# A two-level Winograd-style matrix product: the four raw products moved to the front, and the outer weight sums made partly by adding DMAs in DRAM

## The reference

```python
base  = einsum('bsi,oi->bso', x, weight) + bias        # one weight, 2048 x 2048
low   = einsum('bsi,bri->bsr', x, lora_a[itok7])       # rank 16, one of 8 adapters per batch
delta = einsum('bsr,bor->bso', low, lora_b[itok7])
x = x + base + scale[itok7] * delta
w = L1_weight[itok14]                                  # one of 16 weights per batch
x = x + einsum('bij,bkj->bik', x, w)
```

## Time and profile before

| | us |
|---|---|
| median of 3 runs | 2579.33 (2576.03 to 2581.75) |
| the profiled execution's own time | 2576.68 |
| its span | 2574.9 |
| TensorE busy | 2557.1 (99% of the span) |
| VectorE busy | 2114.2 (82%) |
| ScalarE busy | 1386.3 (54%) |
| GpSimd busy | 764.6 (30%) |
| DMA | 686.19 MB, mean 266 GB/s |

### The profile page before, as it was taken

How to read it: one execution, slowest core, us unless ns; L and a number is a source line. 1 busy time by engine, 2 the same in 40 slices (tenths; PEclk the granted TensorE clock), 3 DMA queues, 4 the chain that set the end, 5 groups by cost and what they waited for, 6 DMA issues and landing times.

```text
span 2574.9 us, 35471 instructions
## 1 busy us (share of the span) xinstructions
PE 2557.1 (99%) x12250; PEld 2114.8 (82%) x12250; DVE 2114.2 (82%) x1926; ACT 1386.3 (54%) x1478; POOL 764.6 (30%) x614
## 2 busy tenths in 40 slices
PE   8999999999999999999999999999999999999999
PEld 7888888888888888878888888888888888888887
DVE  6568999997888999898788787788877887887865
ACT  3324333334344333467676676766766666766755
POOL 5554332332333324220230231311311312212312
PEclk9999999999999999999999999999999999999999
DMA  9996642963576637878678677787899999998986
GB/s 357 352 379 197 203 135 99 290 213 131 162 239 216 168 131 242 308 264 280 243 258 297 240 263 279 247 278 260 290 355 355 353 349 365 353 324 320 312 325 228
DMA packets 213714, 686.19 MB, mean 266 GB/s; under 512 B 23424, under 2 KB 31776, under 8 KB 213536
## 3 DMA queue, kind: packets, MB, share of 16 engines
q1 hardware_dynamic: 204032, 649.33, 70.0%
q0 software_dynamic: 9216, 33.56, 6.7%
q10 hardware_dynamic: 288, 1.05, 0.1%
HBM read 650.29 MB, written 100.66 MB: 292 GB/s over the span
## 4 chain that ended last, share of the span: by engine, by line
PE 92%; DVE 4%; DMA 2%; issue 1%; ACT 0%; SPq 0%; POOL 0%; DVEq 0%; ACTq 0%; POOLq 0%
PE acc L1294 18%; PE acc L1295 18%; PE acc L1296 18%; PE acc L1211 12%; PE acc L1213 12%; PE acc L1212 12%; DVE tx L1165 1%; DVE ws L1165 1%; PE acc L1228 1%; PE acc L1250 1%; DMA bias_s<-bias 1%; DMA xb<-x_sums 1%; DMA xst<-xt 0%; DVE acc L1154 0%; DMA xb<-x 0%
## 5 line engine op out<-in xcount | busy, mean ns | idle before, releaser
L1165 DVE TENSOR_TENSOR ws<-wb,ws 128x1024 fp32r<-128x1024 f32 x968 | 1257.0, 1325 | 284.0 <-ACT ws L1001 268.2
L1001 ACT CAST ws<-wb 128x1024 fp32r<-128x1024 f32 x968 | 990.9, 1050 | 778.3 <-PE acc L1296 450.7
L1294 PE MATMUL acc<-ws,ops 128*128 128x512 f32 (+1 forms) x2048 | 799.9, 391 | 2.6 <-DVE ops L1165 2.3
L1295 PE MATMUL acc<-ws,ops 128*128 128x512 f32 (+1 forms) x2048 | 797.6, 389 | 0.0
L1296 PE MATMUL acc<-ws,ops 128*128 128x512 f32 (+1 forms) x2048 | 797.2, 389 | 0.0
L911 POOL TENSOR_TENSOR wb<-wb,eye_s 128x128 f32<-128x128 f32 x384 | 332.2, 897 | 1145.5 <-DMA wb<-w 1144.9
L1211 PE MATMUL acc<-tx,ws 128*128 128x512 f32 x1600 | 623.5, 390 | 4.5 <-DVE tx L1165 2.4
L1212 PE MATMUL acc<-tx,ws 128*128 128x512 f32 x1600 | 622.5, 389 | 0.0
L1213 PE MATMUL acc<-tx,ws 128*128 128x512 f32 x1600 | 622.5, 389 | 0.0
L1294 PEld LDWEIGHTS acc<-ws,ops 128*128 128x128 f32 x2048 | 384.6, 188 | 82.5 <-issue 6.2
L1296 PEld LDWEIGHTS acc<-ws,ops 128*128 128x128 f32 x2048 | 384.5, 188 | 81.0
(11 more groups left out here) (67 smaller groups left out, 1021.0 us busy)
## 6 DMA issues: line engine op xcount, KB each, us to landing
wb<-w SPq DMA_DIRECT2D x816, 512.0 KB, 6.8
xb<-x SPq DMA_DIRECT2D x78, 512.0 KB, 5.7
xb<-x POOLq DMA_DIRECT2D x64, 512.0 KB, 8.8
y<-acc SPq DMA_DIRECT2D x32, 1024.0 KB, 10.4
wb<-w_sums SPq DMA_DIRECT2D x64, 512.0 KB, 7.9
out<-ost SPq DMA_DIRECT2D x128, 256.0 KB, 7.4
xst<-xt SPq DMA_DIRECT2D x60, 512.0 KB, 6.4
ystage<-y SPq DMA_DIRECT2D x60, 512.0 KB, 7.3
```

Of the source, the lines that this page charges most:

```text
L1001: eng.copy(hi, src).then_inc(s_hi, 1)
L1165: eng.tensor_tensor(lo, src, hi, ALU.subtract).then_inc(s_lo, 1)
L1294: eng.matmul(dst, yh, wh, start=begin, stop=False)
L1295: eng.matmul(dst, yh, wl, start=False, stop=False)
```

## The change

Five things change together.

1. The outer products run in another order: (group 0, k = 0), (0, 1), (1, 0), (1, 1), then k = 2 to 6 of group 0, then k = 2 to 6 of group 1. These first four take raw weight quarters.
2. Only the first of them is `Eight` (`PLAIN = (0,)`), so there are 8 + 13 x 7 = 99 steps.
3. The partial result of (1, 0) stands in slot 1 as "P", is stored in a new DRAM tensor `x_part` (4 blocks of 1 MB), and comes back to slot 2 before outer product (1, 3) adds to it (`part_back`).
4. Of the four outer weight sums GpSimd makes only two parts per tile place, each a difference of two raw tiles (a21 - a22 and a11 - a12 of the outer quarters). For the other three sums, SyncE copies a11 from DRAM to DRAM (`base_sum`, 16 copies of 512 KB) for sums 1 and 2, sum 3 starts from GpSimd's second difference, and 24 adding DMAs issued by GpSimd ("more", three rounds of eight, DRAM to DRAM, 512 KB each) add the rest. The copies are due from 74 us on, the adding DMAs from 104 us on, 6.5 us apart.
5. `MADE_EVERY` goes from 18 to 12 us.

```diff
-SLOT = ({"X": 0, "Y": 1, "Q": 2, "Z": 1}, {"X": 2, "Y": 1, "Q": 0, "Z": 1})
-TARGET = ("X", "Y", "Q", "X", "X", "Z", "X")
+ORDER = [(0, 0), (0, 1), (1, 0), (1, 1)] + [(g, n) for g in range(NG) for n in range(2, K)]
+GRP, NUM = zip(*ORDER)
+POS = {gn: q for q, gn in enumerate(ORDER)}
+SLOT = ({"X": 0, "Y": 1, "Q": 2, "Z": 1}, {"P": 1, "X": 2, "Y": 2, "Q": 0, "Z": 1})
+TARGET = (("X", "Y", "Q", "X", "X", "Z", "X"), ("P", "Y", "Q", "X", "X", "Z", "X"))
...
-MADE_AS = (2, 0, 1, 3)
+MADE = ((1, "m1", 0), (2, "m2", 3))
 MADE_FROM = 10.0
-MADE_EVERY = 18.0
+MADE_EVERY = 12.0
+ADD_FROM = 104.0
+ADD_EVERY = 6.5
...
-PLAIN = (0, 1)
+PLAIN = (0,)
...
-        for i, after in ((1, 3.0), (0, 6.0), (2, 9.0), (3, 12.0)):
-            loads.append((made_key(p) + after, "keep", (p, i)))
+        for n in range(2):
+            loads.append((made_key(p) + 3.0 + 3.0 * n, "keep", (p, n)))
+            loads.append((ADD_FROM - 30.0 + 4.0 * (8 * n + p), "base", (n + 1, p)))
...
-        for i, kind in enumerate(("m1", "m2", "m3", "m4")):
-            adds.append((made_key(p) + 3.0 * i, kind, (p,)))
+        for n in range(2):
+            adds.append((made_key(p) + 3.0 * n, MADE[n][1], (p,)))
+        for n in range(1, 4):
+            adds.append((ADD_FROM + ADD_EVERY * (8 * (n - 1) + p), "more", (n, p)))
...
+    for blk in range(4):
+        loads.append((ev_key(last_step(POS[1, 0], blk), 3) + 6.0, "store", (1, "P", blk)))
+        loads.append((t_of(BEGIN[POS[0, 6]] + 4) + 11.0 * blk, "back", (blk,)))
...
+        def sum_stored(eng, n, p):
+            if n == 0:
+                made_kept(eng, p, 0)
+            else:
+                eng.wait_ge(s_more[p], 16 * n)
...
             def load_made(p, i):
                 if p >= 2:
-                    made_kept(eng, p - 2, i)
-                    eng.wait_ge(s_pool, pool_no["m4", p - 2])
+                    eng.wait_ge(s_pool, pool_no[MADE[i // 2][1], p - 2])
+                    if i in (1, 2):
+                        made_kept(eng, p - 2, i - 1)
...
+            def base_sum(n, p):
+                eng.dma_start(w_sum(n, p), w_part(0, 0, p)).then_inc(s_base[n - 1], 16)
...
+            def part_back(blk):
+                stored(eng, 0, "Q", blk)
+                stored(eng, 1, "P", blk)
+                eng.dma_start(acc[:, SLOT[1]["X"], blk, :], x_part[blk]).then_inc(s_back[blk], 16)
...
+                if kind == "more":
+                    n, p = index
+                    if n == 3:
+                        made_kept(eng, p, 1)
+                    else:
+                        eng.wait_ge(s_base[n - 1], 128)
+                    if n > 1:
+                        eng.wait_ge(s_more[p], 16 * (n - 1))
+                    if n != 2:
+                        made_kept(eng, p, 0)
+                    eng.dma_start(w_sum(n, p), w_part(1, 0, p) if n == 2 else w_sum(0, p), accum_op=ALU.add,
+                                  max_dma_last_dim=4096).then_inc(s_more[p], 16)
+                    continue
...
-                elif kind in ("m1", "m2", "m3", "m4"):
+                elif kind in ("m1", "m2"):
                     p, = index
...
+                    i = 0 if kind == "m1" else 2
+                    made_loaded(eng, p, i)
+                    made_loaded(eng, p, i + 1)
+                    ins = eng.tensor_tensor(made_tile(p, 1 if i == 0 else 2), made_tile(p, i), made_tile(p, i + 1),
+                                            ALU.subtract)
...
                     elif k == 3 and opens:
-                        ev_done(eng, last_step(K * g, blk), ot)
+                        if g:
+                            eng.wait_ge(s_back[blk], 16)
+                        else:
+                            ev_done(eng, last_step(POS[g, 0], blk), ot)
```

More of the change, by code:

```diff
@@ L35 @@
 LEAD = 13.0
+XS_AHEAD = 6.0
 X_ROLE = {"b11": (0, 0), "b12": (0, 1), "b21": (1, 0), "b22": (1, 1)}
@@ L90 @@
 BEGIN = [STEPS.index((q, 0)) for q in range(NG * K)]
-MADE = [(role, h) for role in FORM[2].w_need for h in range(2)]
+TILES = [(role, h) for role in FORM[POS[0, 2]].w_need for h in range(2)]
 def last_step(q, blk):
@@ L364, in program @@
     for _, kind, index in adds:
-        if kind != "acc":
+        if kind not in ("acc", "more"):
             count += 1
@@ L374, in program @@
             for ot in range(4):
-                (fast if q % K in (0, 2) and i in FORM[q].first else slow).append((ev_key(s, ot), s, ot))
+                (fast if NUM[q] in (0, 2) and i in FORM[q].first else slow).append((ev_key(s, ot), s, ot))
     fast.sort()
@@ L555, in ev_done, with stored, free_slot @@
             eng.wait_ge(s_copy if (s, ot) in by_copy else s_ev, ev_no[s, ot])
+        def stored(eng, g, name, blk):
+            eng.wait_ge(s_y0[SLOT[g][name]][blk], 16 * STORES[g, name])
+        def free_slot(eng, g, name, blk):
+            if (g, name) in FREE_BEHIND:
+                stored(eng, *FREE_BEHIND[g, name], blk)
         def blk_view(slot, blk):
@@ L778, in _ @@
                     keep_made(*index)
+                elif kind == "base":
+                    base_sum(*index)
                 elif kind == "store":
                     store_y0(*index)
+                elif kind == "back":
+                    part_back(*index)
                 elif kind == "raw":
@@ L811, in _ @@
                         y0_stored(0)
+                        y0_stored(1)
+                        for blk in range(4):
+                            stored(eng, 0, "Q", blk)
                     elif b == 0:
@@ L856, in _ @@
                     v = w_tile(q, role, h).rearrange("p (s n) -> p s n", s=2)[:, :, 256 * h:256 * h + P]
-                    ins = eng.tensor_tensor(v, v, eye_s[:], ALU.add if UNIT[q % K] > 0 else ALU.subtract)
+                    ins = eng.tensor_tensor(v, v, eye_s[:], ALU.add if UNIT[NUM[q]] > 0 else ALU.subtract)
                 elif kind == "s1":
@@ L969, in _ @@
                         for blk in range(4):
-                            eng.wait_ge(s_y0[2][blk], 32)
+                            stored(eng, 1, "X", blk)
                     else:
@@ L1081, in _ @@
                     x, q, z = (blk_view(SLOT[g][name], blk)[:, :, cols] for name in ("X", "Q", "Z"))
-                    s = last_step(K * g + (3 if what == "z" else 4), blk)
+                    s = last_step(POS[g, 3 if what == "z" else 4], blk)
                     ev_done(eng, s, 2 * oh + 1)
@@ L1177, in _ @@
             for i in range(WARM):
-                eng.matmul(bank[0][:], tx[:, 0, 0, 0:P], tx[:, 0, 0, 0:512], start=True, stop=True)
+                eng.matmul(bank_at(0, 0)[:], tx[:, X_SLOT[0], 0, 0:P], tx[:, X_SLOT[0], 0, 0:512], start=True, stop=True)
             for blk in blocks:
@@ L1187, in _ @@
                         eng.wait_ge(s_key, 10)
-                        eng.matmul(bank[6][:, 0:NB], wide, put, start=True, stop=True).then_inc(s_put, 1)
+                        eng.matmul(order_at[:, 0:NB], wide, put, start=True, stop=True).then_inc(s_put, 1)
                     if blk == ("W", 1, 2):
```

132 lines of the change are left out of this document (66 added, 66 removed).

## The result

The changed kernel takes 2581.73 us (median of 20 runs, 2579.17 to 2584.23), the kernel before 2577.7 us (20 runs, 2576.03 to 2581.75). The ratio is 1.0014, with a 95% interval of 1.0008 to 1.0020. It is slightly slower, within the 0.2% that the prediction called no change. The forecast of 2567.4 us and the range up to 2577 us were wrong: one step less was bought, and it brought nothing. Its profiled execution has a span of 2578.8 us, 3.9 us over before.

What follows compares the result with a forecast made beforehand. TensorE was taken as the bound: matmul count times pace, plus its waits. −10.9 − 1.5 + 0.5 = −11.9 us took the median 2579.33 to 2567.4 us, range 2562 to 2577.

Steps and rivals of the forecast that it cites:

- One step less: Outer product 1 no longer plain: 48 matmuls fewer on TensorE at 0.2267 us each, −10.9 us.
- Sixteen GpSimd sums fewer: Early outer sums dropped, so VectorE runs freer between 33 and 70 us: −1.5 us, bounds 0 and −2.3.
- VectorE in outer product 1: VectorE's added splits and additions fit, 64.7 of 76 us busy: +0.5 us, bounds 0 and +3.
- GpSimd's list ahead of outer product 1: Second s2 behind all 16 differences and the last raw tile, near 108 us, still in time: 0 us, bound +3.
- Rival A: Last raw tile lands at 118 us or later, stalling TensorE 7 to 11 us: about 2576 us, chance 0.12.
- The copies: Sixteen DRAM copies; first eight land near 120 us, before the s4 behind the first adding DMA may start: covered.
- The adding DMAs: 24 adds into DRAM, 1.35 to 5.4 us each, fit the queue before outer product 5: 0 us, bound +6.
- Rival B: Slow DRAM adds stop GpSimd's list above 9.4 us each; at 12 us each, 2601 us, chance 0.13.
- The partial result: 4 MB stored and read back, the read starting some ten steps before its user: 0 us.
- C: Small new stalls in Sevens during busy DMA, VectorE losing 3 to 6 us in sum: 2571 to 2574, chance 0.15.

Runs made afterwards that it cites:

- Experiment 10: Changed kernel with early reads of the partial result and GpSimd's differences of tile places 5 to 7 on 8 of 1024 columns (result incomplete): 2569.77 us, before 2578.01.
- Experiment 2: Changed kernel with GpSimd's differences of tile places 5 to 7 on only 8 of 1024 columns (result incomplete): 2578.06 us, before 2578.03.
- Experiment 6: Changed kernel with early reads of the partial result, differences of places 5 to 7 at 176 to 207 us, adding DMAs from 185 us, copies moved along: 2614.09 us.
- experiment 4: Changed kernel with outer product 1 plain again, one step more, all else as changed: 2587.78 us, before 2578.03.
- experiment 3: Changed kernel with the partial result's reads some 50 us later and differences of places 5 to 7 on 8 of 1024 columns (result incomplete): 2575.31 us, before 2578.03.
- experiment 1: Changed kernel with the four 1 MB reads of the partial result issued some 50 us later: 2580.06 us, before 2578.03.
- experiment 5: Changed kernel with three reads of the partial result issued early, the fourth after the x saves of outer product (1, 2); full result: 2574.74 us, before 2578.2.
- experiment 8: Kernel before, plus four DRAM copies of 1 MB where the changed kernel reads the partial result; nothing waits for them: 2587.86 us, before 2578.33.
- experiment 7: Changed kernel with early reads, differences of places 5 to 7 due at 143, 168 and 224 us, adding DMAs from 205 us: 2598.6 us, before 2578.33.
- experiment 9: Changed kernel with early reads, differences of places 5 to 7 at 143, 168, 220 us, adding DMAs regrouped by place before 310 us: 2584.68 us, before 2577.94.

## Why the prediction was wrong

**One step less, −10.9 us: right.** TensorE has 48 matmuls fewer. Experiment 10 shows most of the gain once both places are relieved: −8.2 us, with 3.5 us of waits left at the first.

**Sixteen GpSimd sums fewer, −1.5 us: right in kind, too small.** All 2.3 us of waits from 30 to 100 us went. VectorE's collisions moved with the sums that stayed.

**VectorE in outer product 1, +0.5 us with a bound of +3: the first step that failed.** It was 5.3 us of waits. The 64.7 us of a like outer product held no differences of GpSimd. The prediction had this outer product and the last six differences in the same 30 us, in two separate steps: one priced VectorE without GpSimd, the other priced GpSimd's list against its due time. The bound allowed one or two collisions. Six differences from 87 to 118 us, at 2.2 us a collision as the earlier trace rows has it, give up to 13 us. That sum was never made, and the slack was taken over all 76 us: where the two met, from 87 to 119 us, VectorE was busy 28.7 of 32 us. Experiment 2 took away the waits up to 130 us by thinning the differences and nothing else. Experiment 6 took all of it away by moving them, with other transfers, and experiment 4 by making the outer product plain.

The lock that the Trainium skill describes on "SBUF — State Buffer" (the section on the two separate sides) agrees with the 1.2 and 3.4 us. The prediction worked it out only for the collisions that left; those that came had a bound and no count.

**GpSimd's list ahead of outer product 1, 0 us: right for the changed kernel.** The last raw tile landed at 114.9 us (forecast 108, bounds 104 and 116, so near the late end), the last difference was done at 118.3 us, and the second s2 then waited for VectorE and not for data. Experiment 10 shows how thin the reserve was: with VectorE on time, tiles that landed at 119 us were part of a wait of 3.5 us. Rival A was a real mechanism, in a kernel that the prediction did not have before it.

**The copies, 0 us: right in the sum, but not covered as thought.** The eighth landed at 126.3 us and not near 120, the first adding DMA was issued at 126.6 us, and GpSimd had stood still for 2.4 us before it. The s4 behind it then waited 3.4 us for VectorE, so nothing was lost. Once the differences were thin, the same wait came to the front (experiments 2, 3 and 10), and in experiment 6 it was 7.2 us.

**The adding DMAs, 0 us: right for the changed kernel.** The changed kernel's software queue from 112 to 270 us:

```profile
q0 software_dynamic: 3267, 11.94, 39.8%
```

That is 62.9 us of all engines for 11.94 MB, 5.3 us a MB or 2.8 us a transfer. Adding into DRAM costs what adding into SBUF did (5.1 us a MB), and the 2.7 us taken was near. GpSimd never waited for an earlier round, and TensorE was busy for all of 180 to 300 us. What the prediction left out is GpSimd's order of work: adding DMAs fill the gaps between its operations, beside the long splits of experiments 2, 3, 4, 6 and 10. Rival B, with its limit of 9.4 us an add, was far off.

**The partial result, 0 us: the second and larger step that failed.** It was 8.0 us of waits. The prediction asked whether the reads would come in time for their own user, ten steps later, and they did. It did not ask what stands behind them on the queues: eight saves of x tiles, for which VectorE's combinations wait. That these had no reserve was in the trace of before (VectorE waited 2.7 and 3.7 us for them) and in no row that the prediction quotes. Experiments 1, 5 and 8 show it from three sides.

**Rivals.** None named the two places. C came nearest in kind at the first place, VectorE late in a Seven, but priced it at 3 to 6 us and had nothing at 700 us.

The sum closes when it is counted from start to start of the matmuls, 0.227 us apart where nothing waits. The idle time of the profile is less than a wait costs, since the first matmuls behind a wait also start later. So counted, the changed kernel differs from before by −10.9 us for the step, −2.8 us from 30 to 100 us, +6.6 us from 100 to 150 us, +0.4 us from 340 to 680 us, +10.2 us from 680 to 765 us (some 1.5 us of it slow clock, below) and +0.3 us in all the rest. This gives +3.8 us, and the spans differ by 3.9 us. What makes the wait of 0.9 to 1.3 us near 685 us, in most of the kernels with the new order, stays open.

A small slip: the low end of the range, worked out as 10.9 + 2.3 us and 3 us of scatter under 2579.3 us, is 2563 and not 2562. It changes nothing.

## What to carry to other kernels

Price a moved transfer by what stands behind it on its queue, not only by its own due time; the consumer to ask for is the one whose wait is already half a step long. When work of two engines that hinder each other moves, add their busy times over the stretch where they meet, not over the whole outer product, and compare the sum, collisions included, with the slack there. And where the queues are full, a transfer moved out of one wait makes the next. Of the five new sets of due times (experiments 1, 5, 6, 7 and 9), one won. It put the transfers ahead of an idle stretch of the queues, so that they had landed before the next saves were issued.

## What the runs showed of the hardware that was not expected

A VectorE operation with two SBUF inputs is not held up for one operation of GpSimd only. While GpSimd ran six without a gap, with adding DMAs between them, one split lasted 16.98 us (1.2 us alone, experiment 6). Beside two s4 and the adding DMAs around them a split took 6.9 us (experiments 2 and 10). Whether issuing a DMA holds VectorE too, or only leaves it no gap, no run shows.

TensorE's clock fell after some of its waits. After 3.6 us without matmuls at 731 us, the next eight started 0.43 us apart (0.56 us between the first two) and not 0.23, half the rate, 1.2 in place of 2.4 GHz. The granted clock of 735 to 745 us is the 0.84 ahead of the DMA share in this row (windows of the changed kernel):

```profile
735.00:745.00 10.00, 10.00 (x38) 8.15 (x39) 3.73 (x4) 4.97 (x8) 0.00 (x0) 0.84 1.03 413
```

By the spacing this cost some 1.5 us. After the 1.7 us wait at 725 us nothing of the kind shows. After waits of 2.4 us it went both ways with the same program: at 128 us the granted clock stayed full in the changed kernel and in experiment 5, and in experiment 1 it was 0.57 from 127 to 131 us.
